# A gated four-layer transformer with experts: the second half's norm at three layer entries, with tokens in partitions

## What is computed

```python
def _layernorm(x, axis=-1, eps=1e-05):
    m = jnp.mean(x, axis=axis, keepdims=True)
    v = jnp.var(x, axis=axis, keepdims=True)
    return (x - m) / jnp.sqrt(v + eps)
...
x = x + tanh(g_xattn[0]) * L0_xattn(layernorm(x), ctx, ctx)     # decayed running sum
x = x + tanh(g_ffn[0])   * L0_ffn(layernorm(x), ...)            # 8 experts of 512, gelu, top 2
x = x + tanh(g_xattn[1]) * L1_xattn(layernorm(x), ctx, ...)     # attention, 16 heads of 8
x = x + tanh(g_ffn[1])   * L1_ffn(layernorm(x), ...)            # 8 experts of 352, silu gated, top 2
x = x + tanh(g_xattn[2]) * L2_xattn(layernorm(x), ...)          # additive attention, tanh of sums
x = x + tanh(g_ffn[2])   * L2_ffn(layernorm(x), ...)            # 16 experts of 128, top 4 of 2 groups
x = x + tanh(g_xattn[3]) * L3_xattn(layernorm(x), ctx, ctx, ...)
x = x + tanh(g_ffn[3])   * L3_ffn(layernorm(x), ...)            # 8 experts of 512 and a shared one, top 2
```

## Time and profile before

| | |
|---|---|
| median of 3 runs | 599.48 us (597.36 to 603.2) |
| profiled execution | 601.89 us, span 600.1 us |
| PE busy | 566.8 us, 94% |
| PEld busy | 394.1 us, 66% |
| DVE busy | 447.4 us, 75% |
| ACT busy | 415.2 us, 69% |
| POOL busy | 103.8 us, 17% |
| chain that ended last | PE 71%, DVE 14%, ACT 10%, issue 3%, POOL 1% |

### The profile page before, as it was taken

One profiled execution on the slowest core, in us unless ns is written; L12 is line 12 of the kernel. 1 busy time (PEld: TensorE's weight loads), 2 busy tenths in 40 slices (PEclk: granted clock), 3 DMA queues, 4 the chain that ended last, 5 costly groups with the idle time before them and its releaser, 6 DMA issues.

```text
span 600.1 us, 8818 instructions
## 1 busy us (share of the span) xinstructions
PE 566.8 (94%) x3305; PEld 394.1 (66%) x3310; DVE 447.4 (75%) x696; ACT 415.2 (69%) x579; POOL 103.8 (17%) x69
## 2 busy tenths in 40 slices
PE   7999999989999999999896989999998999999997
PEld 5688787656677777775230436566545777888886
DVE  4378987588657898987989676766766847787786
ACT  4798999756755556647999765534513858888885
POOL 5400000001200000003989703200000210000000
PEclk9999999999999999999999799999998999999999
DMA  6207210200200811020000024505510110812100
GB/s 237 71 12 307 71 35 2 74 2 2 76 0 4 317 55 58 2 70 1 5 1 1 1 71 120 164 2 153 163 35 2 37 37 0 301 52 72 37 0 35
DMA packets 16782, 40.27 MB, mean 67 GB/s; under 512 B 1834, under 2 KB 6058, under 8 KB 16740
## 3 DMA queue, kind: packets, MB, share of 16 engines
q1 hardware_dynamic: 16740, 39.71, 19.9%
HBM read 39.01 MB, written 0.70 MB: 66 GB/s over the span
## 4 chain that ended last, share of the span: by engine, by line
PE 71%; DVE 14%; ACT 10%; issue 3%; POOL 1%; DVEq 0%; ACTq 0%; POOLq 0%
PE ps L713 38%; ACT work L1094 6%; PE ps L756 4%; PE ps L452 3%; DVE h_lo L1609 2%; PE ps L469 2%; PE ps L739 2%; PE ps L584 2%; PE ps L741 2%; PE ps L555 2%; PE ps L740 2%; PE ps L569 2%; PE ps L459 2%; PE ps L695 2%; DVE h_act L1586 1%
## 5 line engine op out<-in xcount | busy, mean ns | idle before, releaser
L1609 DVE TENSOR_TENSOR h_lo<-h_act,h_hi 128x512 fp32r<-128x512 f32 (+1 forms) x136 | 118.4, 874 | 39.8 <-ACT h_hi L1139 39.0
L713 PE MATMUL ps<-n_hi,w_hi 128*128 128x512 f32 (+1 forms) x232 | 85.4, 402 | 2.0 <-DVE h_act L1586 1.3
L1139 ACT CAST h_hi<-h_act 128x1024 fp32r<-128x1024 f32 (+1 forms) x88 | 75.3, 856 | 14.6 <-PE ps L713 12.1
L713 PE MATMUL ps<-n_hi,w_lo 128*128 128x512 f32 (+1 forms) x232 | 83.0, 391 | 0.0
L713 PE MATMUL ps<-n_lo,w_hi 128*128 128x512 f32 (+1 forms) x232 | 83.0, 391 | 0.0
L1817 POOL TENSOR_TENSOR rstd<-var_eps,minus_half 128x4 f32<-128x4 f32 x16 | 17.5, 1093 | 319.4 <-DVE var_eps L1273 319.4
L713 PE MATMUL ps<-h_hi,w_hi 128*128 128x512 f32 (+1 forms) x184 | 65.5, 398 | 0.1
L713 PE MATMUL ps<-h_hi,w_lo 128*128 128x512 f32 (+1 forms) x184 | 64.0, 390 | 0.0
L713 PE MATMUL ps<-h_lo,w_hi 128*128 128x512 f32 (+1 forms) x184 | 63.9, 389 | 0.0
L1094 ACT ACTIVATE work<-work,p_rest 128x2048 f32<-128x2048 f32 x31 | 59.5, 1998 | 0.4 <-DVE work L1468 0.4
L1132 ACT ACTIVATE h_act<-ps 128x512 f32<-128x512 f32 (+1 forms) x48 | 28.6, 596 | 40.4 <-PE ps L713 40.4
(11 more groups left out here) (234 smaller groups left out, 1023.7 us busy)
## 6 DMA issues: line engine op xcount, KB each, us to landing
work<-g_rows SPq DMA_DIRECT2D x36, 512.0 KB, 6.4
w_f<-in_w SPq DMA_DIRECT2D x20, 512.0 KB, 3.6
w_f<-in_w SPq DMA_DIRECT2D x8, 544.0 KB, 3.6
work<-in_w SPq DMA_DIRECT2D x2, 512.0 KB, 4.3
work<-g_rows SPq DMA_DIRECT2D x4, 256.0 KB, 9.7
p_rest<-in_p_rest SPq DMA_DIRECT2D x1, 714.0 KB, 9.8
p_attn<-in_p_attn SPq DMA_DIRECT2D x1, 546.5 KB, 6.9
x<-in_xT SPq DMA_DIRECT2D x1, 512.0 KB, 3.6
```

The source lines that it names most:

```text
L713: mm = pe.matmul(dst[i], wap(wt, e, lo, size, rows), mv[i], start=(first and c == 0), stop=(last and c == 2))
L1139: act.copy(places(h_hi, m, step), places(h_act, m, step)).then_inc(s["hi"], 1)
L1609: dve.tensor_tensor(lo, src, hi.bitcast(F32), ALU.subtract).then_inc(s["lo"], 1)
```

## The change

For the second half of norms 1, 3 and 7 the norm is made with tokens in partitions. PE turns x by four transposes (`norm_turn`, into bank 5); DVE takes mean and variance of each 128-token tile (four `bn_stats`, four `bn_aggr`, then the add of epsilon: `norm_stats`); POOL's power is as before; DVE subtracts the mean and multiplies with rstd, both now scalars per partition, in four operations from PSUM into the free second half of `sq` (`norm_rows`); PE turns the result back by four transposes (`norm_back`); ACT copies it out of PSUM twice, cast to `n_hi` and plain to `n` (`norm_turned`).

Gone for these halves are the mean, variance and spread on PE, the square, the copy to `xc` and the cast of n on ACT, and the product on DVE. The first halves and the other norms stay.

The order changes with it. On PE the turn stands where the mean stood, and norm_back stands in the experts ahead of the last up before the second logits (layers 0 and 3: ahead of up(3); layer 1: ahead of up(2), and the logits move behind up(2)). On ACT norm_turned stands in step 1, behind the casts of steps 0 and 1 (in layer 1 behind the cast of step 0). On DVE norm_rows stands behind the first `advance()`, which is low(0) in layers 0 and 3 and the first product in layer 1; a second `advance()` stands ahead of norm_low and the routing. In layers 0 and 3 that is one step more ahead of the routing than before.

```diff
@@ semaphores and lists
+        n_rows = sq[:, HALF:T]
+        TURNED = [(j, 1) for j in (1, 3, 7)]
+        SPREAD = [(j, t) for j in range(8) for t in range(2) if (j, t) not in TURNED]
+        def nth_norm(j, t):
+            return (TURNED if (j, t) in TURNED else SPREAD).index((j, t)) + 1
@@ PE
+            def norm_turn(j):
+                pe.wait_ge(x_done[1], j)
+                for i in range(HT):
+                    mm = pe.transpose(ps[:, 5, i * P:(i + 1) * P], x[:, HALF + i * P:HALF + (i + 1) * P], ident)
+                mm.then_inc(ln["turn"], 1)
+            def norm_back(j):
+                pe.wait_ge(ln["rows"], nth_norm(j, 1))
+                for i in range(HT):
+                    mm = pe.transpose(ps[:, 5, i * P:(i + 1) * P], n_rows[:, i * P:(i + 1) * P], ident)
+                mm.then_inc(ln["back"], 1)
             def norm_rest(j):
                 norm_spread(j, 0)
-                norm_mean(j, 1)
+                norm_turn(j)
...
                 logits(MOES[j // 2], 0)
-                norm_var(j, 1)
-                pe.wait_ge(ln["xc"], 2 * j + 2)
@@ PE, moe: layer 1
                     up(0)
-                    norm_spread(3, 1)
                     up(1)
+                    norm_back(3)
+                    up(2)
                     logits(m, 1)
-                    up(2)
@@ PE, moe: layers 0 and 3
                     up(1)
                     if L == 0:
                         prepare_values(0, 2)
-                    else:
-                        norm_spread(7, 1)
                     up(2)
+                    norm_back(2 * L + 1)
                     up(3)
                     logits(m, 1)
@@ PE, prologue
-            norm_mean(1, 1)
+            norm_turn(1)
             norm_spread(1, 0)
-            norm_var(1, 1)
             prepare_keys(0, 1, 0)
             prepare_keys(0, 1, 1)
-            norm_spread(1, 1)
             pe.wait_ge(pre["kcp"], 3)
             logits(MOES[0], 0)
@@ ACT
+            def norm_turned(j):
+                act.wait_ge(ln["back"], nth_norm(j, 1))
+                act.copy(n_hi[:, half(1)], ps[:, 5]).then_inc(ln["hi"], 1)
+                act.copy(n[:, half(1)], ps[:, 5]).then_inc(ln["n"], 1)
             def norm_rest(j):
                 norm_high(j, 0)
-                norm_square(j, 1)
-                norm_copy(j, 1)
@@ ACT, moe
                 high(0)
-                norm_high(2 * L + 1, 1)
...
+                    if step == 1:
+                        norm_turned(2 * L + 1)
@@ DVE
+            def norm_stats(j):
+                dve.wait_ge(ln["turn"], nth_norm(j, 1))
+                for i in range(HT):
+                    ins = dve.bn_stats(bn[:, i], ps[:, 5, i * P:(i + 1) * P])
+                link(ins)
+                for i in range(HT):
+                    ins = dve.bn_aggr(mv[:, i], bn[:, i])
+                link(ins)
+                dve.tensor_scalar(var_eps[:, HT:], mv[:, :, 1], EPS, None, ALU.add).then_inc(ln["eps"], 1)
+            def norm_rows(j):
+                dve.wait_ge(ln["rstd"], 2 * j + 2)
+                for i in range(HT):
+                    ins = dve.tensor_scalar(n_rows[:, i * P:(i + 1) * P], ps[:, 5, i * P:(i + 1) * P],
+                                            mv[:, i, 0:1], rstd[:, HT + i:HT + i + 1], ALU.subtract, ALU.mult)
+                ins.then_inc(ln["rows"], 1)
@@ DVE, moe
                 norm_out(j, 0)
                 norm_low(j, 0)
-                norm_eps(j, 1)
+                norm_stats(j)
+                advance()
+                norm_rows(j)
                 if m.gated:
-                    advance()
-                    norm_out(j, 1)
                     low(0)
-                    norm_low(j, 1)
-                    advance()
-                else:
-                    norm_out(j, 1)
-                    advance()
-                    norm_low(j, 1)
+                advance()
+                norm_low(j, 1)
                 differences()
                 route(m, advance)
```

More of the change, by code:

```diff
@@ L183, in flamingo @@
         rstd = sb("rstd", [P, TILES])
+        bn = sb("bn", [P, HT, 6])
+        mv = sb("mv", [P, HT, 2])
+        n_rows = sq[:, HALF:T]
         rt = {k: sb(f"rt_{k}", [P, TILES * 16]) for k in ("lg", "cur", "e", "top8", "above", "equal", "rank", "chosen", "w")}
@@ L253, in flamingo @@
         x_done = [sem("x_done0"), sem("x_done1")]
-        ln = {k: sem(f"ln_{k}") for k in ("mean", "xc", "sq", "var", "eps", "rstd", "bc", "n", "hi", "lo")}
+        ln = {k: sem(f"ln_{k}") for k in ("mean", "xc", "sq", "var", "eps", "rstd", "bc", "turn", "rows", "back", "n", "hi", "lo")}
         pre = {k: sem(f"pre_{k}") for k in ("kv", "scan", "proj", "k", "v", "vcp", "kcp", "txt", "txtcp", "uv", "uvcp", "uv_dram", "uv_in", "wo")}
@@ L454, in norm_var @@
             def norm_var(j, t):
-                pe.wait_ge(ln["sq"], 2 * j + t + 1)
+                pe.wait_ge(ln["sq"], nth_norm(j, t))
                 for i in range(HT):
@@ L465, in norm_spread @@
                 if LNBANK[j, t][2] == LNBANK[j, t][0]:
-                    pe.wait_ge(ln["xc"], 2 * j + t + 1)
+                    pe.wait_ge(ln["xc"], nth_norm(j, t))
                 for i in range(HT):
@@ L885, in _ @@
             prepare_keys(0, 0, 1)
-            norm_mean(1, 1)
+            norm_turn(1)
             norm_spread(1, 0)
-            norm_var(1, 1)
             prepare_keys(0, 1, 0)
             prepare_keys(0, 1, 1)
-            norm_spread(1, 1)
             pe.wait_ge(pre["kcp"], 3)
             logits(MOES[0], 0)
-            pe.wait_ge(ln["xc"], 4)
+            pe.wait_ge(ln["xc"], 3)
             moe(MOES[0], {36: [lambda: norm_mean(2, 0)], 37: [lambda: norm_var(2, 0)], 39: [lambda: norm_spread(2, 0)], 41: [lambda: queries(0, 0)]})
@@ L913, in norm_square @@
             def norm_square(j, t):
-                act.wait_ge(ln["mean"], 2 * j + t + 1)
+                act.wait_ge(ln["mean"], nth_norm(j, t))
                 act.activation(sq[:, half(t)], ps[:, LNBANK[j, t][0]], ACT.Square).then_inc(ln["sq"], 1)
@@ L1245, in _ @@
             copy_keys(0, 0, 1)
-            norm_square(1, 1)
-            norm_copy(1, 1)
             split_hi_up(MOES[0], 1)
@@ L1271, in norm_eps @@
             def norm_eps(j, t):
-                dve.wait_ge(ln["var"], 2 * j + t + 1)
+                dve.wait_ge(ln["var"], nth_norm(j, t))
                 dve.tensor_scalar(var_eps[:, t * HT:(t + 1) * HT], ps[:, LNBANK[j, t][1], 0:HT], EPS, None, ALU.add).then_inc(ln["eps"], 1)
             def norm_out(j, t):
-                dve.wait_ge(ln["bc"], 2 * j + t + 1)
-                dve.wait_ge(ln["xc"], 2 * j + t + 1)
+                dve.wait_ge(ln["bc"], nth_norm(j, t))
+                dve.wait_ge(ln["xc"], nth_norm(j, t))
                 dve.tensor_tensor(n[:, half(t)], xc[:, half(t)], ps[:, LNBANK[j, t][2]], ALU.mult).then_inc(ln["n"], 1)
+            def norm_stats(j):
[13 more added lines that the diff above has]
+                ins.then_inc(ln["rows"], 1)
             def norm_low(j, t):
                 dve.wait_ge(ln["hi"], 2 * (j // 2) + t + 1)
+                if (j, t) in TURNED:
+                    dve.wait_ge(ln["n"], 2 * j + 2)
                 dve.tensor_tensor(n_lo[:, half(t)], n[:, half(t)], n_hi[:, half(t)].bitcast(F32), ALU.subtract).then_inc(ln["lo"], 1)
@@ L1731, in advance @@
                         if L == 3 and step == 9:
+                            dve.wait_ge(ln["n"], 2 * 7 + 2)
                             dve.scalar_tensor_tensor(x[:, :], n[:, :], tg[:, 7:8], x[:, :], ALU.mult, ALU.add).then_inc(s["xn"], 1)
```

## The result

| | kernel before | with the change |
|---|---|---|
| median | 601.04 us (597.36 to 603.2) | 606.64 us (605.1 to 610.69) |
| ratio, 95% interval | | 1.0120 (1.0086 to 1.0154) |
| profiled execution | 601.89 us, span 600.1 | 606.53 us, span 604.7 |

The median before is that of four executions, the three ahead of the prediction and one of 602.6 us more. The change makes the kernel slower by 1.2% by the ratio, some 7 us; the two medians of four lie 5.6 us apart. The forecast was 599.3 us, no change, and the time lies outside its range.

What follows compares the result with a forecast made beforehand. The chain of waits was taken to run almost wholly through PE up to the turned gates, with DVE last in layer 3. Layers 0, 1 and 3 summed -0.59 - 0.66 + 1.05 = -0.20, giving 599.3 us, range 597.0 to 603.0.

Steps and rivals of the forecast that it cites:

- D: Rival: PE's clock falls in new holes, 1.67 and 0.6 us in layer 3; once 601.0, all three layers 604.4; chance 0.15.
- the evidence taken "against": Against the clock rival: granted clock 1.00 over 130 to 160 us, a stretch full of transposes and short waits.
- Nothing between the entries is bound by a fixed time: Between the changed layer entries: weights, gate rows and updates follow from the same steps, so the entries' shifts sum to -0.20.
- Layer 0, forecast -0.59: Layer 0's entry: PE turns the gates at 38.73 instead of 39.32 us, 0.59 earlier.
- The loss at the fourth low: Layer 0's routing: the fourth low now needs the sixth cast instead of the fifth; 0.85 us lost.
- POOL's three w_lo subtractions start 1 us later, so nothing: Layer 0, behind POOL's power: down(0), first to want them, came more than 5 us after them; no cost.
- my upper end: norm_rows on DVE, each changed layer: 0.91 us taken for four operations, at most 4 x 0.28 = 1.12 without overlap.
- C: Rival: DVE's new work is dear, bn_stats and bn_aggr 0.8 + 0.5 more, norm_rows 1.12; 601.7 us, chance 0.24.
- Layer 1, forecast -0.66: Layer 1's entry: turned gates about 0.66 us earlier, DVE and PE balanced there.
- Layer 3, forecast +1.05: Layer 3's entry: logits at 499.68 instead of 498.63 behind norm_rows, norm_back and copies; turned gates 1.05 us later.
- A: The forecast itself: PE's saved time eaten by waits for norm_rows and the copies; gain, gain, loss; 599.3 us, chance 0.50.
- B: Rival: the whole PE saving arrives, 3 x 1.77 = 5.3 us, giving 594.1; chance 0.06.

Runs made afterwards that it cites:

- the filling of the old holes alone: The change with bf16 matmuls nobody reads filling PE's old holes at 114, 126, 131 and 455 us, new holes open; 1.0081 against the kernel before.
- the layer alone: Kernel before with only layer 1's second half (norm 3) turned, norms 1 and 7 as before; ratio 0.9990 (0.9967 to 1.0013).
- all holes filled: The change with unread bf16 matmuls filling PE's old holes and its own new ones in layers 0 and 3; 1.0042 against the kernel before.
- 0.9 us late: Kernel before with four bf16 filling matmuls more ahead of layer 0's turned gates, norms untouched; ratio 1.0097 (1.0058 to 1.0136).
- 3.4 us late: Kernel before with sixteen bf16 filling matmuls more ahead of layer 0's turned gates, norms untouched; ratio 1.0085 (1.0062 to 1.0108).

## Why the prediction was wrong, point by point

**The clock (D): right in kind, failed in two terms.** D was priced at 1.67 and 0.6 us holes in layer 3, 1.7 us a fall and one fall likely if any, and got 0.15. Layer 3's fall came as described, once. The first failed term is the evidence taken "against": 1.00 over 130 to 160 us was read as proof that short holes are harmless there. It was one execution at one arrival time: in the kernel before with its gates 0.9 us later, 135 to 140 us has 0.66. The second is the place: the prediction looked for falls only in the **new** holes, while of the measure's 10.2 us the filling of the old holes alone took 3.3 and that of the new ones, on top, another 2.4 (on two chips, each with a standard error of about 1). So "Nothing between the entries is bound by a fixed time", with which a shift at one entry was carried to the end unchanged, failed there. D in full, 604.4 by its three falls, was the nearest of the four times; the change measured 606.6.

**Layer 0, forecast -0.59, profiled +0.9 at the gates.** In the kernel after, up(0) was at 22.39 (forecast 22.14) and low(0) at 24.73 (24.52): well forecast. Then norm_rows starts 1.04 behind low(0) instead of 0.61, and takes 1.35 instead of 0.91. PE:

```profile
27.18 0.66 PE L492 MATMUL ps<-p_first,sq 128*128 128x128 f32 x4 [1.25 <-DVE sq L1315]
...
29.00 1.06 PE L500 MATMUL ps<-p_attn,n 128*128 128x8 f32 x8 [0.47 <-ACT n L946]
```

The forecast took the old gates at 39.32, from the chain; their row starts at 39.16, so that by it the forecast was -0.43. norm_back was at 27.18 instead of 26.08, logits at 29.00 instead of 27.83: their gain of 1.02 was gone. The loss at the fourth low is as worked out and arrived in full: it waits 0.87 for the sixth cast and starts at 35.82, where the earlier trace rows have 34.73. The step that failed is "POOL's three w_lo subtractions start 1 us later, so nothing". They were priced by who waits for them, not by who runs beside them: in the kernel before, DVE does an operation with a PSUM operand beside them, now two lows.

**norm_rows.** Four take 1.35 us, 395 to 403 ns each and 0.32 from start to start; my upper end was 1.12. That end assumed the 0.28 of an operation without overlap, from one whose operands aren't in PSUM. The 1.03 estimated from the Trainium skill (VectorE: DVE Perf Modes, the TRN2 errata) was nearer than my 0.91 and still short by 0.32.

**Statistics (C).** bn_stats 0.88 for four (forecast 0.91), bn_aggr 0.38 (0.3), the add 0.17 (0.16), and norm_rows follows low without waiting for POOL: right. C had the larger chance than D, and only its smaller term, norm_rows, came true.

**Layer 1, forecast -0.66, profiled 0.0.** up(0) is 1.1 earlier against the arrival, as forecast. Then:

```profile
177.78 0.66 PE L492 MATMUL ps<-p_first,sq 128*128 128x128 f32 x4 [1.29 <-DVE sq L1315]
...
179.64 1.02 PE L500 MATMUL ps<-p_rest,n 128*128 128x8 f32 x8
```

The idle time is 1.29 instead of 0.98, and DVE, the limit behind it, carries norm_rows' 0.44 more. The remaining 0.2 I haven't traced. That the term was near nothing is borne out by the layer alone, 0.9990.

**Layer 3, forecast +1.05, profiled +2.6 at the gates** against the arrival there. In the kernel after:

```profile
496.19 0.50 PE L734 MATMUL ps<-n_hi,w_hi 128*128 128x512 f32 x1 [0.32 <-DVE n_lo L1323]
...
499.09 1.36 DVE L1315 TENSOR_SCALAR sq<-ps,mv,rstd 128x128 f32<-128x128 f32 x4
...
500.50 0.66 PE L492 MATMUL ps<-p_first,sq 128*128 128x128 f32 x4 [1.97 <-DVE sq L1315]
...
501.68 0.59 ACT L946 COPY n<-ps 128x512 f32<-128x512 f32 x1
...
502.32 1.06 PE L500 MATMUL ps<-p_rest,n 128*128 128x8 f32 x8 [0.47 <-ACT n L946]
```

Every hop is where it was put: norm_rows behind low(0), PE idle ahead of norm_back 1.97 (1.67 forecast, the difference being mostly norm_rows), another 0.47 (0.6 forecast), logits late by 1.6 against the arrival (1.05 plus norm_rows' 0.44). The remaining 0.9 is the fall at 503 to 507 us: with the holes filled the gates are late by 1.7, not 2.6.

**The sum.** At full clock the forecast was -0.2; measured are between +1.2 (the change, its clock measure taken off) and +2.7 (all holes filled). Three times 0.44 for norm_rows and, as an estimate, 0.5 to 1 for DVE beside POOL would carry most of it, so A was near at the steps and missed the time by what hangs on them. The rest is the clock: 6.0 of 7.2 us by the measure, 4.5 by what filling the holes brought back. B was rightly held unlikely.

## What to carry to other kernels

A row of granted clock 1.00 over a stretch with short waits says that they were harmless at this one alignment; look for holes of about 1 us in the whole span, not only at the edit, and take a clock term for every one of them as soon as the edit moves the work by a microsecond. One profiled execution doesn't say where a kernel's falls lie: average the clock over many. To tell a delay from a fall, delay the old kernel by the same amount with filling work. And price an operation that is moved by what the other engines do beside it, not only by who waits for it.

## What the runs showed of the hardware

- Whether the clock falls behind an existing hole hangs on when the work arrives: 0.9 us late, 5.1 us of clock measure more; 3.4 us late, 0.3. From where the lateness is to be counted isn't settled; from the span's start it isn't (116.03 us without a fall, 116.08 with one). The 0.9 us of span that the 3.4 us delay cost beyond itself is not explained.
- Beside POOL's subtractions of two SBUF operands (1.25 us each alone), a DVE subtraction of two SBUF operands of 128x512 takes 1.12 to 1.70 us instead of 0.69, and POOL's three take 4.18 instead of 3.76. Where DVE's started 0.04 us ahead, it took 0.69 and POOL's 1.80. DVE operations with an operand in PSUM were not slowed.
- bn_stats on 128x128 from PSUM takes 280 ns, four 0.88 us; bn_aggr 148 ns, four 0.38; subtract and multiply by two scalars per partition from PSUM 400 ns, four 1.35.
